# The batch loop's first instruction: aligned to 256 instruction slots on five engines, not on TensorE alone

## What is computed

```
xn = layernorm(x)
q  = relu(xn @ Wq.T + bq);  k = relu(keys @ Wk.T + bk);  v = relu(values @ Wv.T + bv)
a  = softmax(q_h k_h.T / 4) v_h        for each of the 16 heads
f  = clip(xn @ sign(Wf).T * scale + bias, -100, 100)
out = x + (a + xn) + f
```

## Time and profile before

| | |
|---|---|
| median of 3 runs | 2848.66 us (2847.84 to 2852.46) |
| the profiled execution | 2850.59 us, of which the span from the first to the last instruction is 2848.8 us |
| TensorE busy (matmul) | 2770.7 us, 97% of the span |
| ScalarE, VectorE, GpSimd busy | 2450.2 us (86%), 2337.4 us (82%), 938.4 us (33%) |
| mean granted TensorE clock | 0.983 |

### The profile page before, as it was taken

The page is one execution under the profiler, slowest core; times in us unless marked ns, Lnnn a source line. Parts: engine busy times, 40 slices in busy tenths (PEclk is TensorE's granted clock), DMA queues, the critical chain, the costliest instruction groups (busy, mean ns, idle before and its releaser), DMA issues.

```text
span 2848.8 us, 61155 instructions
## 1 busy us (share of the span) xinstructions
PE 2770.7 (97%) x17860; PEld 1149.8 (40%) x17860; DVE 2337.4 (82%) x4578; ACT 2450.2 (86%) x2949; POOL 938.4 (33%) x845
## 2 busy tenths in 40 slices
PE   8899999999999999999999999999999999999996
PEld 4434444443444434444443444434444443444331
DVE  6788888888888888888888888888888888888940
ACT  4688888888888888888888888888888888888996
POOL 4304334242343314333242343314333242343001
PEclk8699999999999999999999999999999999999998
DMA  7111121121221121121121221121121121211111
GB/s 142 60 40 55 65 70 36 56 70 55 65 70 52 40 70 55 65 66 33 62 69 55 65 66 49 47 70 55 65 64 35 62 68 56 65 62 37 48 55 38
DMA packets 78637, 167.74 MB, mean 59 GB/s; under 512 B 28548, under 2 KB 32647, under 8 KB 76327
## 3 DMA queue, kind: packets, MB, share of 16 engines
q1 hardware_dynamic: 78374, 164.19, 19.2%
HBM read 36.71 MB, written 17.83 MB: 19 GB/s over the span
## 4 chain that ended last, share of the span: by engine, by line
PE 79%; issue 10%; DVE 7%; ACT 2%; POOL 1%; DVEq 0%; DMA 0%; POOLq 0%; ACTq 0%
PE value_ps L611 30%; PE ring L633 28%; PE score_ps L597 13%; DVE mx L959 5%; ACT probs L806 2%; PE score_ps L677 1%; PE score_ps L662 1%; PE score_ps L679 1%; PE score_ps L666 1%; PE score_ps L664 1%; PE ring L720 1%; POOL fin L1097 1%; PE score_ps L715 0%; DVE excess L934 0%; PE ring L700 0%
## 5 line engine op out<-in xcount | busy, mean ns | idle before, releaser
L806 ACT ACTIVATE probs<-score_ps 128x1024 f32<-128x1024 f32 x2048 | 1992.3, 1024 | 236.1 <-PE score_ps L597 229.9
L959 DVE TENSOR_REDUCE mx<-ring 128x1 f32<-128x512 f32 x2952 | 1900.1, 684 | 248.8 <-PE ring L633 224.5
L633 PE MATMUL ring<-kstack,qstack 48*128 48x512 f32 x3444 | 1168.4, 467 | 16.7 <-DVE mx L959 3.1
L611 PE MATMUL value_ps<-probs,vones 128*32 128x512 f32 x8192 | 1092.3, 605 | 1.1 <-ACT taken L813 0.4
L633 PEld LDWEIGHTS ring<-kstack,qstack 48*128 48x128 f32 x3444 | 490.1, 184 | 1071.0 <-DVE mx L959 1034.3
L597 PE MATMUL score_ps<-qstack,kstack 51*128 51x512 f32 x4096 | 814.1, 416 | 13.8 <-ACT probs L806 4.5
L934 DVE CUSTOM_DVE_ANT_0 excess<-ring,excess 128x512 f32<-128x512 f32 x512 | 353.1, 690 | 136.7 <-PE ring L633 119.1
L1097 POOL TENSOR_TENSOR dense<-dense,affine 128x512 f32<-128x512 f32 x128 | 164.4, 1284 | 866.7 <-ACT dense L856 865.2
L597 PEld LDWEIGHTS score_ps<-qstack,kstack 51*128 51x128 f32 x4096 | 393.6, 186 | 132.1 <-ACT probs L806 70.5
L822 ACT ACTIVATE excess<-ring 128x512 f32<-128x512 f32 x492 | 294.0, 597 | 1.4 <-PE ring L633 1.2
L611 PEld LDWEIGHTS value_ps<-probs,vones 128*32 128x32 f32 x8192 | 161.5, 108 | 320.7 <-issue 289.1
(11 more groups left out here) (93 smaller groups left out, 1417.2 us busy)
## 6 DMA issues: line engine op xcount, KB each, us to landing
qstack<-parts SPq DMA_DIRECT2D x768, 64.0 KB, 2.5
fin<-taken SPq DMA_DIRECT2D x256, 128.0 KB, 2.9
xin<-x SPq DMA_DIRECT2D x16, 1024.0 KB, 5.1
base_cur<-base_new SPq DMA_DIRECT2D x16, 1024.0 KB, 5.3
fin<-recip SPq DMA_DIRECT2D x32, 512.0 KB
out<-fin SPq DMA_DIRECT2D x32, 512.0 KB, 2.6
qstack<-proj SPq DMA_DIRECT2D x256, 12.0 KB
kstack<-base_cur SPq DMA_DIRECT2D x16, 128.0 KB, 6.0
```

The lines of the kernel that those rows point to most:

```text
L611: mm = pe.matmul(value_ps[h4 * 32:(h4 + 1) * 32, :], vones[:, 2 * tp + c, hh * HALF + side * PAIRS + 2 * g + j, :, :], probs[:, q % 2 * GR ...
L633: pe.matmul(ps[:, :], qstack[nh][rows, pair, st * P:(st + 1) * P], keys, start=True, stop=True).then_inc(s_mm, 1)
L806: nc.scalar.activation(probs[:, q % 2 * GROUP + u % GROUP, :], score_ps[src][:, :], ACT.Exp, scale=EXP_SCALE).then_inc(s_probs, 1)
L959: nc.vector.tensor_reduce(most, src[:, :], AX.X, ALU.max).then_inc(s_mx, 1)
```

## The change

The parameter `aligned` goes, and the mark is put into the stream of every engine that calls `run`, at the same place: behind the first half step written out, ahead of the loop's MOVE.

```diff
-        def run(eng, half_step, aligned=False):
+        def run(eng, half_step):
...
             half_step(0, 1, True, (0, 0), None, False, True)
-            if aligned:
-
-                eng.addr_align(256)
+
+            eng.addr_align(256)
             with nc.Fori(1, NB - 1, engines=bass.OrderedEngineSet([eng.engine]), hint_back_edge=True) as b:
                 half_step(b, 0, True, (b - 1, 1), (b - 1, 0), True, False)
                 half_step(b, 1, True, (b, 0), (b - 1, 1), False, True)
...
-            run(pe, half_step, aligned=True)
+            run(pe, half_step)
```

## The result

| | before | after |
|---|---|---|
| median | 2851.16 us (6 runs) | 2862.01 us (6 runs, 2861.47 to 2863.59) |
| profiled execution, span | 2848.8 us | 2860.1 us |
| mean granted clock | 0.983 | 0.981 |

The ratio is 1.0046 with a 95% interval of 1.0035 to 1.0056: 0.46% slower, which is 13 us with an interval of 10 to 16. The forecast was 17.4 us more, 2866.1 us.

The account below looks back on a forecast made before the run. The prediction took TensorE, busy for 97% of the span, to bound the kernel. A 15.1 us stop plus 2.3 for the clock, with 0 for other engines and back edges, made 17.4 on 2848.66: 2866.1 us, range 2854 to 2874.

Parts of the forecast that it names:

- The mechanism: At the loop's entry, VectorE's executed padding stops TensorE and the clock falls: 15.1 + 2.3 us.
- the fourth matmul of the ring: First TensorE matmul into the three banks needing VectorE's new reduction; claimed at 217.0 instead of 201.9 us, 15.1 us late.
- The number of NOPs: Padding at the loop's entry, to multiples of 256 slots: VectorE 241, ScalarE 139, GpSimd 101, SyncE 40, TensorE nothing new.
- The price of a NOP: Spacing of NOPs at the entry, taken from TensorE: 72 ns, bounds 13 to 90, so 17.4 us of padding on VectorE.
- the step's own formula: TensorE's delay at the entry: 241 c - 2.3 us, with c the time per NOP on VectorE.
- its own signs: Stated checks: NOP counts per engine, 72 ns spacing, VectorE's first reduction near 216 us behind over 15 us idle, turns of 171.3 us.
- The sign on the place: The whole difference must be found between 198 and 235 us, or the explanation fails.
- The clock term: Behind TensorE's stop at the entry: 5 us of work at half clock cost 2.3 us, bounds 0 to 4.5.
- ScalarE beneath VectorE: At the entry, ScalarE's 10.0 us of padding runs beside VectorE's and adds 0; alone it would cost some 6 us.
- The back edges: At the 13 returns to the loop's head, alignment gains 0, with 8.1 us as the bound.
- stepped over: Rival: the four engines branch over unused slots at the entry, 2848.7 us; chance 0.14 together with very cheap NOPs.
- faster: Rival: the 13 back edges end last on VectorE and padding is jumped over, 8.1 us saved, 2840.6 us; chance 0.04.

Follow-up runs that it names:

- VectorE alone: The kernel before with the mark on VectorE as well as TensorE, not on the other three engines: 2862.17 us against 2849.98, ratio 1.0045.
- the doses: The kernel before with other marks on VectorE only: 111 NOPs 2856.89 us (against 2849.51), 120 NOPs 2859.96 and 494 NOPs 2874.04 (both against 2849.13).
- ScalarE alone: The kernel before with the mark on ScalarE as well as TensorE, not on the other three engines: 2854.91 us against 2849.98, ratio 1.0017.
- the kernel that jumps: The kernel before with the mark on the four new engines at a maximum of 0 NOPs, so unused slots are branched over: 2851.46 us against 2849.98, ratio 1.0006.

## Why the prediction was right, and where it wasn't
**The mechanism held.** Padding is executed, VectorE's decides, it has one queued reduction to hide it, TensorE stops at the fourth matmul of the ring, the clock falls, nothing is made up later and the turns stay the same. VectorE alone costs as much as all four, GpSimd and SyncE cost nothing, and the alignment without NOPs earns nothing.

**The number of NOPs** was 241, 139, 101 and 40; it was 239, 137, 103 and 54. The loader's own instructions are then 64, 64, 60 and 48 slots, not 62 on each engine. On VectorE that is 1%. That the mark pads to slots of 256 is shown by the doses: slot 137 in place of slot 0 took 119 NOPs off VectorE's 239 (256 - 137 = 119, and 120 remained), slot 128 took 128 off (111 remained), and slot 255 asked for behind slot 0 added 255.

**The price of a NOP was mis-sized**, and that is nearly the whole miss. I took TensorE's 72 ns for VectorE, and my bounds from rows, 13 to 90, held its 48. It was the only NOP in the trace, but of another engine, and a comparison of register additions (40 against 32 ns) led upward when the truth was below. The MOVE and the hint on VectorE that seemed to confirm it last 44 and 56 ns themselves, where a NOP lasts 13 to 18, so they said little of a NOP. The stop came out as 9.5 us where 15.1 stood: 239 x 48 ns - 2.3 = 9.2. So the step's own formula carries it, with the 0.3 to 0.4 us between the last NOP and the MOVE (210.0 and 210.4) that I had not seen. By its own signs the forecast was thus off here: the spacing was to be near 72 ns, and VectorE's first reduction near 216 us behind more than 15 us of idle time; it came at 210.70 behind 11.02. That the time still fell into the range is due to a range that had room for cheaper NOPs. The sign on the place held: 11.0 of the 11.3 us are found between 198 and 235 us.

**The clock term** (the trace gives the clock as a share, 1.00 ahead of the fall and 0.50 behind it, and no row gives it in GHz) was 2.3 us with 5 us at half clock; it was 1.8 with 4.0 by the same reckoning, and 1.5 by the timelines. I had read the fall from the end of the run, 5 us behind the last matmul, and it came at 205.1, 3.2 us after TensorE had first run dry at 201.9. ScalarE alone showed how wide I should have held this term: there it was 3.1 us of 4.9.

**ScalarE beneath VectorE** was right: 1.74 us of its wait stand in the changed kernel and cost nothing there. Alone it would not have been the 6 us that the forecast named for it, but 2.0 and the clock: a NOP of 41 ns again.

**The back edges** were right for these engines. The kernel with no mark shows that a loop head's place can cost 1.6 us of waiting at each back edge, on the engine that was aligned already. That an alignment might earn something at the branch itself was only my supposition, and no run shows it. The rivals "stepped over" and "faster" fall with the rows of L373 and with the kernel that jumps.

## What to carry to other kernels
Try the alignment of a loop's head on the engine that issues the most instructions per microsecond and bounds the loop (here TensorE, 2663 in 171 us, where no mark cost 40 us), and look at the others first: here none of the other four gained anything at a back edge by it (ratio 1.0006 without the NOPs). A mark was paid in NOPs where it stood, 19 to 255 of them here, so put it where that engine waits anyway, as in the kernel with the mark at the head of TensorE's stream (19 NOPs beneath a wait until 9.97 us), and ask for the slot that brings the loop's head to the boundary. When an engine that feeds TensorE stops for a few microseconds, add the clock to the stop: with 111 and 120 NOPs on VectorE the stop was 3.1 and 3.6 us and the clock 4.6 and 4.5, with 239 it was 9.5 and 1.8.

## What the runs showed of the hardware that I had not expected
- In the changed kernel a NOP came every 72 ns on TensorE and every 38 to 48 ns on the other four engines.
- A stop of TensorE of 1.75 us, shortly behind one of 1.3 us, was followed by a fall of the granted clock from 1.00 to 0.50, for 6.9 us of full work; the one of 1.3 us alone was not, in the kernel before. Of the 13 stops of about 1.6 us in the kernel with no mark, five were.
- With its loop entered at slot 237 of 256, TensorE stood still for 1.6 us shortly behind each of the 13 back edges: 40 us over the run with what the clock added. VectorE's loop head at slot 111, 17 slots ahead of the end of a piece of 128 by my estimate, cost nothing (2849.27 us against 2849.13).
- The slot of VectorE's loop head still has an effect: at slot 10 each turn was 171.47 and 171.48 us long, at slot 1 it was 171.27, at slot 111 (2595.5 - 368.9) / 13 = 171.28. The reason is open.
